# Recommender tower on one core: layer two with samples on the output partitions, layer three on VectorE

## The reference

```python
e = jnp.stack([tbl_0[ids[:, 0]], ..., tbl_26[ids[:, 26]]], axis=1)   # [2048, 27, 128]
dot_products = jnp.einsum('bnd,bmd->bnm', e, e)
z = dot_products[:, c, r]                       # the 351 pairs below the diagonal
h = jnp.concatenate([z, dense_ctx], axis=1)     # 367
h = jnp.maximum(h @ W_top1 + b_top1, 0.0)       # 512
h = jnp.maximum(h @ W_top2 + b_top2, 0.0)       # 256
y = h @ W_top3                                  # 1
```

## Time and profile before

| | us |
|---|---|
| Median of 3 runs | 508.99 (507.92 to 510.58) |
| The profiled execution | 516.17 |
| Its span | 514.2 |
| PE busy in the span | 409.3 |
| POOL busy | 264.1 |
| DVE busy | 223.1 |
| ACT busy | 171.8 |
| PE's granted clock, mean share of full speed | 0.907 |

### The profile page before, as it was taken

The page is one execution under the profiler, slowest core; times in us unless marked ns, Lnnn a source line. Parts: engine busy times, 40 slices in busy tenths (PEclk is TensorE's granted clock), DMA queues, the critical chain, the costliest instruction groups (busy, mean ns, idle before and its releaser), DMA issues.

```text
span 514.2 us, 9233 instructions
## 1 busy us (share of the span) xinstructions
PE 409.3 (80%) x3024; PEld 381.5 (74%) x3024; DVE 223.1 (43%) x687; ACT 171.8 (33%) x382; POOL 264.1 (51%) x279
## 2 busy tenths in 40 slices
PE   1758887768859978799786969599686987699878
PEld 1647887767849968788776859599586877598866
DVE  3659945344623545335443346235343345342000
ACT  2324223322324323332333323243223333244632
POOL 6766365656653565636563455645564364654000
PEclk9959998798997998899897989799797997989998
DMA  7986314242252314332162312532133321523230
GB/s 180 224 197 184 109 45 125 69 93 70 78 123 50 88 41 113 84 77 74 41 153 50 80 51 56 134 73 77 41 109 75 80 70 35 133 67 83 34 57 1
DMA packets 69933, 45.30 MB, mean 88 GB/s; under 512 B 54854, under 2 KB 58310, under 8 KB 69911
## 3 DMA queue, kind: packets, MB, share of 16 engines
q1 hardware_dynamic: 59577, 26.86, 22.5%
q0 software_dynamic: 8704, 17.84, 13.9%
q10 hardware_dynamic: 1630, 0.31, 0.4%
HBM read 39.02 MB, written 5.98 MB: 88 GB/s over the span
## 4 chain that ended last, share of the span: by engine, by line
PE 68%; issue 10%; another core or an unknown queue 10%; DVE 6%; DMA 3%; ACT 3%; SPq 0%; ACTq 0%; DVEq 0%
PE lookup_ps L489 30%; PE gram_ps L506 20%; PE layer_ps L523 6%; PE gather_ps L474 5%; PE layer_ps L535 5%; DVE one_hot L730 4%; DMA ids_all<-lookup_ids 1%; PE layer_ps L543 1%; DVE table_lo L737 1%; ACT gram L280 1%; DMA gram_dram<-gram 1%; DMA emb<-gram_dram 1%; ACT emb L597 1%; ACT z_hi L611 0%
## 5 line engine op out<-in xcount | busy, mean ns | idle before, releaser
L444 POOL DMA_INDIRECT rows<-tbl,index x272 | 263.3, 968 | 209.2 <-issue 72.6
L730 DVE TENSOR_SCALAR one_hot<-ids_all,row_number 125x256 fp32r<-125x256 int32 x648 | 200.2, 372 | 234.5 <-PE lookup_ps L489 133.1
L489 PE MATMUL lookup_ps<-one_hot,table_hi 125*128 125x256 f32 x640 | 196.8, 333 | 56.2 <-issue 36.0
L489 PEld LDWEIGHTS lookup_ps<-one_hot,table_hi 125*128 125x128 f32 x640 | 134.0, 209 | 71.4 <-issue 53.6
L489 PE MATMUL lookup_ps<-one_hot,table_lo 125*128 125x256 f32 x640 | 175.4, 299 | 1.6 <-issue 1.4
L506 PE MATMUL gram_ps<-emb 128*108 128x108 f32 x1024 | 132.8, 280 | 39.5 <-ACT gram L280 23.3
L506 PEld LDWEIGHTS gram_ps<-emb 128*108 128x108 f32 x1024 | 123.2, 194 | 43.0 <-ACT gram L280 24.7
L489 PEld LDWEIGHTS lookup_ps<-one_hot,table_lo 125*128 125x128 f32 x640 | 134.3, 210 | 1.3 <-issue 1.1
L280 ACT COPY gram<-gram_ps 108x432 f32<-108x432 f32 x128 | 66.5, 521 | 177.9 <-remote 114.3
L597 ACT ACTIVATE emb<-gather_ps 128x384 f32<-128x384 f32 (+1 forms) x80 | 43.0, 538 | 61.1 <-remote 38.9
L474 PE MATMUL gather_ps<-identity,rows 128*128 128x128 f32 x272 | 45.3, 284 | 1.5 <-ACT emb L597 0.6
(11 more groups left out here) (35 smaller groups left out, 97.0 us busy)
## 6 DMA issues: line engine op xcount, KB each, us to landing
ids_all<-lookup_ids SPq DMA_DIRECT2D x44, 256.0 KB
gram_dram<-gram SPq DMA_DIRECT2D x62, 91.1 KB
emb<-tbl SPq DMA_DIRECT2D x10, 448.0 KB
rows<-tbl,index POOLq DMA_INDIRECT x272
z<-gram_dram SPq DMA_DIRECT2D x14, 117.0 KB
z<-gram_dram SPq DMA_DIRECT2D x7, 104.0 KB
emb<-w SPq DMA_DIRECT2D x3, 192.0 KB
emb<-tbl SPq DMA_DIRECT2D x10, 52.0 KB
```

The lines of the kernel that those rows point to most:

```text
L444: pool.indirect_dma_start(rows[g][:, j * DIM:(j + 1) * DIM], None, tables[f], bass.IndirectOffsetOnAxis(index[p][:, h, f:f + 1], 0)).then_ ...
L489: last = nc.tensor.matmul(lookup_ps[k % LOOKUP_BANKS], table[:, k, row, :], one_hot[u % UNIT_RING][:, r, :], start=(row == 0 and table is ...
L730: last = nc.vector.tensor_scalar(one_hot[u % UNIT_RING][:, r, :], table_ids, row_number[0:LOOKUP_PARTS, row:row + 1], None, ALU.is_equal)
```

## The change

Layer two now takes the activations as the stationary operand and the weights as the moving one, so that the 128 samples of a half lie on the output partitions and the 256 outputs on columns. The number and the size of its matmuls stay. On DVE, two instructions for each half follow: one adds the bias `b2` in PSUM, the next applies relu, multiplies with `w3` and sums along the row, which gives `y` for 128 samples. ACT's `relu2` and `copy_y` and PE's `layer3` are gone; ACT still issues the store of `y`, now from a [128, 2] tile. `b2` and `w3` are loaded as copies on all partitions. SP's `load_z` waits for layer two instead of layer three. The scratch for POOL's DMA descriptors shrinks from 8192 to 4096 bytes per partition.

```diff
-            sp.dma_start(w3_sb[:, :], w3).then_inc(weights_in, 16)
+            sp.dma_start(w3_sb[:, :], w3.partition_broadcast(P)).then_inc(weights_in, 16)
-            sp.dma_start(b2_sb[:, :], b2).then_inc(weights_in, 16)
+            sp.dma_start(b2_sb[:, :], b2.partition_broadcast(P)).then_inc(weights_in, 16)
...
-                sp.wait_ge(l3_full, c + L3_FREE)
+                sp.wait_ge(l2_full, c * HALVES + L2_FREE)
...
             def layer2(c, to):
-                for o in range(o2_tiles):
+                for h in range(HALVES):
                     for k in range(o1_tiles):
...
-                        last = nc.tensor.matmul(layer_ps[o][:, 0:CHUNK], w2_sb[:, k, o * P:(o + 1) * P], to.h1[k],
+                        last = nc.tensor.matmul(layer_ps[h][:, 0:HIDDEN2], to.h1[k][:, h * P:(h + 1) * P], w2_sb[:, k, :],
                                                 start=(k == 0), stop=(k == o1_tiles - 1))
                     last.then_inc(l2_full, 1)
-
-            def layer3(c, to):
-                for k in range(o2_tiles):
-
-                    pe.wait_ge(h2_ready, c * o2_tiles + k + 1)
-                    last = nc.tensor.matmul(layer_ps[0][0:1, 0:CHUNK], w3_sb[:, k:k + 1], to.h2[k],
-                                            start=(k == 0), stop=(k == o2_tiles - 1))
-                last.then_inc(l3_full, 1)
...
-            def relu2(c, to):
-                for o in range(o2_tiles):
-
-                    act.wait_ge(l2_full, c * o2_tiles + o + 1)
-                    nc.scalar.activation(to.h2[o], layer_ps[o][:, 0:CHUNK], ACT.Relu, bias=b2_sb[:, o:o + 1]
-                                         ).then_inc(h2_ready, 1)
-
-            def copy_y(c, to):
-
-                act.wait_ge(l3_full, c + 1 + L3_FREE)
-                nc.scalar.activation(to.y, layer_ps[0][0:1, 0:CHUNK], ACT.Copy).then_inc(y_ready, 1)
-
-                act.wait_ge(y_ready, c + 2)
+            def store_y(c):
+
+                act.wait_ge(y_ready, (c + 2) * HALVES)
                 settle(act)
-                act.dma_start(y_out[bass.ds(c * CHUNK, CHUNK), :].rearrange("b o -> o b"),
-                              to.y).then_inc(y_stored, 16)
+                act.dma_start(y_out[bass.ds(c * CHUNK, CHUNK), :].rearrange("(h p) o -> p (h o)", p=P),
+                              y_sb[:, :], allow_slow_non_contiguous=True).then_inc(y_stored, 16)
...
+            def layer3(c):
+
+                dve.wait_ge(y_stored, c * 16 + DMA_FREE)
+                for h in range(HALVES):
+
+                    dve.wait_ge(l2_full, c * HALVES + h + 1 + L2_FREE)
+                    nc.vector.tensor_tensor(layer_ps[h][:, 0:HIDDEN2], layer_ps[h][:, 0:HIDDEN2], b2_sb[:, :], ALU.add
+                                            ).then_inc(biased, 1)
+
+                    dve.wait_ge(biased, c * HALVES + h + 1)
+                    nc.vector.scalar_tensor_tensor(h2[:, :], layer_ps[h][:, 0:HIDDEN2], 0.0, w3_sb[:, :], ALU.max,
+                                                   ALU.mult, accum_out=y_sb[:, h:h + 1]).then_inc(y_ready, 1)
...
-    nc = bacc.Bacc("TRN2", target_bir_lowering=False, num_devices=1, dynamic_dma_scratch_size=8192)
+    nc = bacc.Bacc("TRN2", target_bir_lowering=False, num_devices=1, dynamic_dma_scratch_size=4096)
```

More of the change, by code:

```diff
@@ L86 @@
 LAYERS_AT = (0.66, 0.80, 0.92)
-Tower = namedtuple("Tower", ["z", "h1", "h2", "y"])
+Tower = namedtuple("Tower", ["z", "h1"])
 def merged(*timed):
@@ L191, in dlrm_tower, with tower @@
         w2_sb = sbuf("w2_sb", [P, o1_tiles, HIDDEN2])
-        w3_sb = sbuf("w3_sb", [P, o2_tiles])
+        w3_sb = sbuf("w3_sb", [P, HIDDEN2])
         b1_sb = sbuf("b1_sb", [P, o1_tiles])
-        b2_sb = sbuf("b2_sb", [P, o2_tiles])
+        b2_sb = sbuf("b2_sb", [P, HIDDEN2])
+        y_sb = sbuf("y_sb", [P, HALVES])
         h1_rest = sbuf("h1_rest", [P, o1_tiles - K_TILES, CHUNK])
-        h2_first = sbuf("h2_first", [P, CHUNK])
+        h2 = sbuf("h2", [P, HIDDEN2])
         spare = emb[0][:, :, :, :].rearrange("p t f s -> p (t f s)").rearrange("p (k b) -> p k b", b=CHUNK)
-        def tower(z_sb, h1_more, h2_one):
-            h1_sb = [z_sb[:, k, :] for k in range(K_TILES)] + [h1_more[:, k, :] for k in range(o1_tiles - K_TILES)]
-            return Tower(z_sb, h1_sb, [h2_one, h1_sb[0]], h1_more[0:1, 0, :])
-        usual = tower(z[:, :, :], h1_rest[:, :, :], h2_first[:, :])
-        final = tower(spare[:, 0:K_TILES, :], spare[:, K_TILES:o1_tiles, :], spare[:, o1_tiles, :])
+        def tower(z_sb, h1_more):
+            return Tower(z_sb, [z_sb[:, k, :] for k in range(K_TILES)] + [h1_more[:, k, :] for k in range(o1_tiles - K_TILES)])
+        usual = tower(z[:, :, :], h1_rest[:, :, :])
+        final = tower(spare[:, 0:K_TILES, :], spare[:, K_TILES:o1_tiles, :])
         gather_ps = [psum(f"gather_ps{i}") for i in range(GATHER_BANKS)]
@@ L242, in dlrm_tower @@
         l2_full = semaphore("l2_full")
-        h2_ready = semaphore("h2_ready")
-        l3_full = semaphore("l3_full")
+        biased = semaphore("biased")
         y_ready = semaphore("y_ready")
@@ L259, in dlrm_tower @@
         L1_FREE = LAYER_BANKS
-        L3_FREE = 1
+        L2_FREE = HALVES
         W1_EVEN = PAIR_ROWS // 16 * 16 - 16
@@ L463, in _ @@
             pe.sem_inc(l1_full, L1_FREE)
-            pe.sem_inc(l3_full, L3_FREE)
+            pe.sem_inc(l2_full, L2_FREE)
             def gather(c, k):
@@ L510, in layer1 @@
             def layer1(c, to):
-                pe.wait_ge(y_ready, c + 1)
+                pe.wait_ge(y_ready, (c + 1) * HALVES)
                 for bank in range(LAYER_BANKS):
@@ L559, in run @@
                         layer2(c0 + c, final if c == N_CHUNKS - 1 else usual)
-                    elif what == "layer3":
-                        layer3(c0 + c, final if c == N_CHUNKS - 1 else usual)
             pe.wait_ge(consts_ready, 2)
@@ L678, in run @@
                         relu1(c0 + c, final if c == N_CHUNKS - 1 else usual)
-                    elif what == "layer2":
-                        relu2(c0 + c, final if c == N_CHUNKS - 1 else usual)
                     elif what == "layer3":
-                        copy_y(c0 + c, final if c == N_CHUNKS - 1 else usual)
+                        store_y(c0 + c)
             def table_high(k):
@@ L718, in _ @@
         def _(dve):
+            dve.sem_inc(y_ready, HALVES)
             def make_unit(c, u):
@@ L756, in run @@
                         split_low(c0 + c, k, final if c == N_CHUNKS - 1 else usual)
+                    elif what == "layer3":
+                        layer3(c0 + c)
             nc.vector.memset(z[:, :, :], 0.0).then_inc(z_cleared, 1)
@@ L778, in _ @@
             run(0, first_steps)
+            dve.wait_ge(weights_in, WEIGHT_LOADS)
             with dve.Fori(0, N_CHUNKS // 2 - 1) as i:
@@ L822 @@
         "w2": np.asarray(inputs["W_top2"]),
-        "b2": columns(inputs["b_top2"]),
-        "w3": columns(inputs["W_top3"]),
+        "b2": np.asarray(inputs["b_top2"]),
+        "w3": np.asarray(inputs["W_top3"]).reshape(-1),
     }
```

5 lines of the change are left out of this document (1 added, 4 removed).

## The result

The changed kernel took 536.66 us (median of 4 runs, 529.36 to 541.47); the kernel before, run beside it, 509.78 us (507.92 to 514.19). I had said 505.9 us, at most 512.5.

What follows compares the result with a forecast made beforehand. PE's own work was taken as the bound, POOL's schedule as a second. Terms +1.6 - 4.5 - 0.2 = -3.1 us took 516.17 to 513.1 profiled, the median to 505.9; range 500 to 512.5, the forecast's own 503 to 506.5.

Steps and rivals of the forecast that it cites:

- The store's price: Last store at the kernel's end, 256 pieces of 4 bytes instead of one of 1 KB: +0.4 us, bounds 0 and +1.6.
- Layer two on PE: PE's layer two: same number and size of matmuls, 3.46 us before, so 0 change.
- Layer three on DVE, 1.75 us: DVE's four new instructions on PSUM per chunk, costed from a row in SBUF: 1.75 us; 2.3 if a quarter dearer.
- 0.95 us given back at the first gram bank: PE's saved layer three lost again waiting for ACT's tenth-table copy behind the store: +1.6 us, bounds -5.7 and +4.9.
- POOL's pull: PE's transposes behind layer three finish earlier, so POOL resumes 1.35 us sooner in five chunks: -4.5 us, bounds 0 and -6.8.
- rival 1: No change: gram bank waits as computed, POOL's pull swallowed by waits for transposes; 510.4 us; chance 0.33.
- the first two terms: The time given back at the first gram bank, +1.6 us, and POOL's pull, -4.5 us.
- SP: SP's `load_z` starts some 2 us sooner, but its data is used half a chunk later: 0.
- scratch: Smaller ring for POOL's indirect DMAs, at most 17 under way: 0 unless it fills.
- ACT's saved activations: Two relus and the copy of `y` leave ACT each chunk, not on the path there: 0.
- Rival 2: Slower: tenth table's copy on ACT waits for DVE, delaying each half's first gram bank; 514.4 us; chance 0.22 with other waits.
- my rule that a signal waits for a burst's end: PE results finished later than some 1.6 us into POOL's indirect-DMA burst reach other engines only about the burst's end.

Runs made afterwards that it cites:

- turned store: Changed kernel, DVE transposing `y` in 32x32 blocks, ACT storing 8 pieces of 128 bytes in two DMAs: 526.55 us, ratio 1.011 (slower kind); 409.51 us, 1.039 (quick kind).
- late store: Changed kernel with `y` transposed on DVE, its store in the loop issued behind ACT's next table copy: 528.20 us, 1.017 (slower kind); 392.93 us, 0.998 (quick kind).
- row store: Changed kernel, ACT storing one 256-value row from one partition, `y` itself not stored; quick kind only: 394.68 us, ratio 1.0046; 396.25 us, 1.0068; 394.68 us, 1.001.
- the pieces in the loop: Changed kernel storing 256 pieces of 4 bytes for the first six chunks, one row for the last two: 404.98 us, ratio 1.0286 (quick kind).
- the kernel before with pieces: Kernel before, its row of `y` stored as 256 pieces of 4 bytes, layer three not moved: 403.36 us, ratio 1.0257 (quick kind).

## Why the prediction was wrong

- *The store's price: the step that failed.* I wrote that its "price lies inside the bounds above and counts only once, at the very end", with bounds of 0 and +1.6 us. Both halves were wrong. At the end it is +7.9 us in the profile (9.5 us behind the issue instead of 1.6), 5.2 us measured alone on the quick kind. And it does not count once: a store also delays other DMAs behind it, 6.6 us at the last chunk's `z` (gone again with the turned store), and the gathers in the loop (queue 0 from 13.9% to 20.1%). The tail's 14.2 us are more than all of the 13.3 us between the two spans, and over half of the 19 to 27 us between the medians. I had bounded the cost by the kernel's own last store and counted the DMA's engine-side issue (0.38 us, right: 0.38 to 0.42), where what counts is the completion.
- *Layer two on PE, 0.* Right, 3.46 us.
- *Layer three on DVE, 1.75 us.* Right, 1.70. The rule of the Trainium skill, "VectorE: DVE Perf Modes", Specifications, that VectorE sits closer to SBUF, showed no price here: 427 ns on PSUM against 427 ns in SBUF.
- *0.95 us given back at the first gram bank.* Right in place and size, and its cause is shown by the late store. From layer two to the gram bank the six places of the changed kernel changed by +0.1, 0.0, 0.0, -0.1, +0.4 and +0.8 us, +1.4 together (rounded from the hundredths), where I had +1.6; the +0.5 of the second place did not come, and the fifth had some of it instead. At the sixth I had +0.9. A drop of the clock behind that pause, 1.45 us where it comes, was not in my sum; it came in some profiles and not in the first one of the changed kernel.
- *POOL's pull, -4.5 us.* Wrong too. The gap shrank to 0.30 us as I said, but POOL waited as much longer for PE's transposes (72.2 to 83.3 us), which is what rival 1 said. The profiled loop came to its last gram records 0.9 us sooner (481.41 against 482.33), where the first two terms make 2.9. The 6 to 10 us that the turned kernels still lose on the slower kind even speak for the opposite sign. On the quick kind, where the kernel before has no such holds, the turned kernel with the late store is even with before. That it is POOL's bursts is argued, not shown: the holds have no releaser in the trace, and their sum differs as much between two runs of one kernel as between kernels.
- *SP, scratch, ACT's saved activations, 0.* Nothing speaks against them; scratch was measured alone.
- *Rivals.* Rival 1 held for POOL's pull. Rival 2's mechanism exists, but in the changed kernel it cost little. The result left the range for a reason that none of the rivals held.

No version tried beats the kernel before; the best, turned with a late store, equals it on the quick kind (0.998) and is 1.7 to 1.9% slower on the other by the ratios, of which the first rests on a set with a wide spread.

## What to carry to other kernels

Before you move a result from one partition to 128, ask how it leaves the chip: a DMA of many tiny pieces was cheap to issue here and short in the packets' own time, and dear in its completion, for itself and for other DMAs under way behind it. Turn the data first (one 0.21 us transpose of 32x32 blocks on DVE did it here) and look, in the profile, for stretches in which nothing runs and something waits for a DMA. And put an issue that waits for another engine behind the work that others wait for on its queue: one place on ACT's list was worth 16.6 us of 394.

## What the hardware showed beyond that

- A store of 256 pieces of 4 bytes has its last packets done about a microsecond after the issue, and the program ends 7.6 to 9.4 us after the issue's end (7.6 and 8.6 on the quick kind, 9.1 and 9.4 on the slower). One row of 1 KB: 1.3 us. Eight pieces of 128 bytes: 1.5 us.
- Chips differ by 30% on this kernel: 394 us against 509 to 520 us, at a granted clock of 0.983 against 0.907 in the profiles of the kernel before. POOL's waits on the slower kind have a line that this kernel and the row store lack altogether on the quick kind; here the kernel before on the first chip:

```profile
POOL rows L444 <- remote: 64.3, 28, 3.1
```

On the quick kind POOL issued for almost 300 us with gaps under 0.5 us, and PE's signals still came through. So my rule that a signal waits for a burst's end describes the slower kind; on the quick one such holds came back only with the pieces in the loop (11.1 us in two copies of ACT, one of 6.8). What makes the difference stays open.
- Pieces in the seventh chunk's store delayed the last `z` loads by 6.6 us on the slower kind and by nothing that could be measured on the quick kind. The sixth chunk's store, though, held back a load of `z` on the quick kind as well, in the kernel before with pieces.
